# Projections from three products of rounded parts, with rows exchanged by transfers within SBUF

## The reference

```python
x = x + gnn(layernorm(x), adj, ...)          # ends in elu(hidden @ W_out + b_out)
h = rmsnorm(layernorm(x), g1)                # [2048, 512]
q, k, v = split(h @ w_qkv, 3)                # w_qkv [512, 1536], fp32
q, k = rope(q, cos, sin), rope(k, cos, sin)  # out_r = xr*c - xi*s, out_i = xr*s + xi*c
y = softmax(causal(q @ k.T / sqrt(32))) @ v  # 16 heads of 32
x = x + y @ w_o
x = x + moe(rmsnorm(x, g2), w_router, w1, w2)   # top 2 of 8 experts, capacity 640
```

## Time and profile before

| | us |
|---|---|
| median of 3 runs | 2176.4 (2174.52 to 2177.14) |
| the profiled execution | 2175.5 |
| its span | 2173.8 |
| TensorE busy | 2023.7 (93%) |
| VectorE busy | 1539.4 (71%) |
| ScalarE busy | 1100.1 (51%) |
| GpSimd busy | 717.8 (33%) |

### The profile page before, as it was taken

How to read it: one execution, slowest core, us unless ns; L and a number is a source line. 1 busy time by engine, 2 the same in 40 slices (tenths; PEclk the granted TensorE clock), 3 DMA queues, 4 the chain that set the end, 5 groups by cost and what they waited for, 6 DMA issues and landing times. The chain is left out here.

```text
span 2173.8 us, 41935 instructions
## 1 busy us (share of the span) xinstructions
PE 2023.7 (93%) x17522; PEld 1202.1 (55%) x17522; DVE 1539.4 (71%) x2484; ACT 1100.1 (51%) x1088; POOL 717.8 (33%) x503
## 2 busy tenths in 40 slices
PE   6899999999999999999999999998991999999997
PEld 3554444444444444554444444444440799999996
DVE  7889999989995766768778778677558544444442
ACT  5778989898893433223454545444440423332321
POOL 3410000000000011335797879877440322222211
PEclk9999999999999999999999999999995999999999
DMA  7421212121213312343104031010222544444431
GB/s 272 155 82 54 72 53 79 49 77 51 74 52 106 138 49 74 140 148 90 40 7 111 21 86 32 25 40 13 76 91 99 189 126 125 99 116 126 126 64 25
DMA packets 92393, 187.70 MB, mean 86 GB/s; under 512 B 14924, under 2 KB 24140, under 8 KB 87820
## 3 DMA queue, kind: packets, MB, share of 16 engines
q1 hardware_dynamic: 83244, 164.04, 22.9%
q0 software_dynamic: 8960, 20.98, 5.2%
HBM read 139.25 MB, written 41.28 MB: 83 GB/s over the span
## 5 line engine op out<-in xcount | busy, mean ns | idle before, releaser
L1782 DVE TENSOR_REDUCE t_rm<-t_m 128x1 f32<-128x512 f32 (+3 forms) x640 | 371.9, 605 | 125.8 <-PE t_m L1923 81.1
L1707 ACT ACTIVATE t_E<-t_s 128x1024 f32<-128x1024 f32 (+3 forms) x320 | 277.3, 895 | 351.9 <-PE t_s L1940 196.3
L629 ACT ACTIVATE m_step<-m_ub,gat_bias 128x2048 bf16<-128x2048 f32 x128 | 250.0, 1989 | 13.9 <-DMA m_ub<-scratch_uac 8.5
L773 PE MATMUL m_bd<-m_mask,m_S 128*32 128x512 bf16 x3072 | 230.3, 379 | 10.9 <-DVE m_mask L719 10.9
L773 PE MATMUL m_bd<-gat_adjT,m_S 128*32 128x512 bf16 x2496 | 201.4, 379 | 4.8 <-PE m_dn L773 4.8
L2135 POOL DMA_INDIRECT out<-e_ye,e_token x40 | 80.7, 2017 | 330.5 <-DVE e_ye L2257 325.8
L966 POOL MEMSET k_triq<- 128x128 bf16 x1 | 0.2, 205 | 572.5 <-POOLq L2391 572.5
L773 PE MATMUL m_bd<-m_mask,m_neg 128*32 128x512 bf16 x2496 | 188.9, 379 | 0.0
L2320 PE MATMUL e_h<-e_xTh,e_w1h 128*128 128x320 f32 x512 | 158.4, 309 | 0.8 <-DVE e_xTl L2236 0.8
L2320 PE MATMUL e_h<-e_xTh,e_w1l 128*128 128x320 f32 x512 | 158.2, 309 | 0.0
L2320 PE MATMUL e_h<-e_xTl,e_w1h 128*128 128x320 f32 x512 | 158.2, 309 | 0.0
(11 more groups left out here) (385 smaller groups left out, 4404.0 us busy)
## 6 DMA issues: line engine op xcount, KB each, us to landing
a_adj<-in_adj SPq DMA_DIRECT2D x16, 1024.0 KB, 5.0
m_ub<-scratch_uac SPq DMA_DIRECT2D x16, 1024.0 KB, 5.0
e_w1r<-in_L_ffn_w SPq DMA_DIRECT2D x8, 2048.0 KB, 9.7
e_w2r<-in_L_ffn_w SPq DMA_DIRECT2D x8, 2048.0 KB, 9.3
tq_Q<-scratch_parts SPq DMA_DIRECT2D x36, 256.0 KB, 4.5
gat_scale<-scratch_uac SPq DMA_DIRECT2D x32, 256.0 KB
scratch_parts<-o_hi SPq DMA_DIRECT2D x32, 256.0 KB, 2.2
scratch_parts<-o_lo SPq DMA_DIRECT2D x32, 256.0 KB, 2.7
```

Of the source, the lines that this page charges most:

```text
L629: act.activation(step(n), ub[h % 2][:, :].rearrange("p (t q) -> p t q", t=T), ACT.Relu, bias=bias[:, j, h:h + 1], scale=BIG).then_inc(step ...
L773: return pe.matmul(out[c * TILE:(c + 1) * TILE, :], lhs, rhs[:, c * BANK:(c + 1) * BANK], **flags)
L1707: act.activation(E[n % 3][:, two, off:BANK], ps_s[:, two, off:BANK], ACT.Exp, scale=SCALE).then_inc(exp_done[z], 1)
L1782: dve.tensor_reduce(rm[:, h, t, ch:ch + 1], ps_m[i % 2][:, 0:w], AX, ALU.max).then_inc(entry_read, 1)
```

## The change

Everything is in stage_front.

- Wr holds the raw weights of w_qkv. ScalarE writes their scaled and rounded high part Wh (weight_high), VectorE the rest Wl (weight_low): 12 pieces of 128x512 each, by the tables HIGHS and LOWS behind the output products. The transposes too are split, into xT[0] by ScalarE and xT[1] by VectorE (turned_low), for two chunks at a time.
- A projection is 12 products (PRODUCTS) with fp32r operands instead of four in fp32. The router's weights G are split into Gs; its products have 16 and 8 columns, into a bank of their own, behind each v item.
- ORDER is another: the Q and K projections of chunk 0 come first, V later; the last chunk ends in qk, qk, v, v. Projections have three banks instead of four.
- The shuffle on VectorE is gone. SP exchanges neighbouring rows from raw to swap with two transfers within SBUF (exchange(n)), and the store of item n-3 stands ahead of it in SP's list. raw has three buffers.
- A rotation follows one item behind its projection, high and low parts two items behind it.
- The tables of cosines and sines are loaded by chunks; load_first stands before item 24.

```diff
-    BANKS = 4
+    BANKS = 3
+    PRODUCTS = ((0, 0), (0, 1), (1, 0))
...
+    ORDER = outs(0, 5) + [("var", 0), ("norm", 0)] + outs(5, 6) + turns(0)[0:2] + outs(6, 7) + turns(0)[2:4] + [qk[0]]
+    ORDER += outs(7, 8) + [qk[1]] + outs(8, 9) + [("var", 1), ("norm", 1), qk[2]] + outs(9, 10) + [qk[3]] + outs(10, 11)
+    ORDER += turns(1) + [qk[4]] + outs(11, 12) + [vs[0]] + outs(12, 13) + [("var", 2), ("norm", 2), qk[5]] + outs(13, 14)
+    ORDER += [vs[1]] + outs(14, 15) + [qk[6]] + outs(15, 16) + [vs[2], qk[7], vs[3]] + turns(2) + [qk[8]]
+    ORDER += [("var", 3), ("norm", 3), vs[4], qk[9], qk[10], vs[5], qk[11], qk[12], vs[6], qk[13], qk[14], vs[7], qk[15]]
+    ORDER += turns(3)
+    for c in (2, 3):
+        q, t = qk[8 * c:8 * c + 8], vs[4 * c:4 * c + 4]
+        ORDER += q[0:2] + t[0:1] + q[2:4] + t[1:2] + q[4:6] + (t[2:3] if c == 2 else []) + q[6:8] + t[3 if c == 2 else 2:]
...
+    HIGHS = {1: ((0, 0), (0, 1)), 2: ((0, 2), (0, 3)), 4: ((1, 0),), 5: ((1, 1),), 6: ((1, 2),), 7: ((1, 3),),
+             8: ((2, 0),), 9: ((2, 1),), 10: ((2, 2), (2, 3))}
+    LOWS = {2: ((0, 0), (0, 1)), 3: ((0, 2), (0, 3)), 6: ((1, 0),), 7: ((1, 1),), 8: ((1, 2),), 9: ((1, 3),),
+            10: ((2, 0), (2, 1)), 11: ((2, 2), (2, 3))}
...
+                def exchange(n):
+                    sp.wait_ge(evicted, PLACE[("qk", n)] + 1)
+                    if n >= 3:
+                        sp.wait_ge(parts_ready, n - 2)
+                    for z in range(2):
+                        sp.dma_start(swap[n % 3][z:P:2, :], raw[n % 3][1 - z:P:2, :]).then_inc(swapped[n % 3], 16)
...
+                for n in range(len(QK)):
+                    if n >= 3:
+                        store(n - 3)
+                        if n in (10, 18):
+                            load_turns(2 + (n - 10) // 8)
+                    if n == 24:
+                        load_first()
+                    exchange(n)
+                for n in range(len(QK) - 3, len(QK)):
+                    store(n)
...
-                    dve.wait_ge(evicted, PLACE[("qk", n)] + 1)
-                    if n >= 3:
-                        dve.wait_ge(parts_ready, n - 2)
-                    lk(dve.stream_shuffle(swap[n % 3][:, :], raw[r][:, :], [d ^ 1 for d in range(32)]))
-                    lk(dve.tensor_tensor(swap[n % 3][:, :], swap[n % 3][:, :], S[:, c * BANK:(c + 1) * BANK], ALU.mult))
+                    dve.wait_ge(swapped[n % 3], 32 * (n // 3 + 1))
+                    dve.wait_ge(cs_in[c % 2], 32 * (c // 2 + 1))
+                    lk(dve.tensor_tensor(swap[n % 3][:, :], swap[n % 3][:, :], S[:, c % 2, :], ALU.mult))
...
+                def weight_low(m, k):
+                    dve.wait_ge(w_high[m], k + 1)
+                    cut = slice(m * D, (m + 1) * D)
+                    dve.scalar_tensor_tensor(Wl[:, k, cut], Wr[:, k, cut], gcol[:, k:k + 1],
+                                             Wh[:, k, cut].bitcast(F32), ALU.mult, ALU.subtract).then_inc(scaled[m], 1)
+
+                def turned_low(n):
+                    dve.wait_ge(t_high, n + 1)
+                    cut = slice(n % 4 * P, (n % 4 + 1) * P)
+                    dve.tensor_tensor(xT[1][:, n // 4 % 2, :, cut], ps_t[n % 2][:, :].rearrange("p (k q) -> p k q", q=P),
+                                      xT[0][:, n // 4 % 2, :, cut].bitcast(F32), ALU.subtract).then_inc(t_ready, 1)
...
                 for kind, n in ORDER:
+                    if kind in ("out", "qk", "v"):
+                        if to_split:
+                            low_part(to_split.pop(0))
+                        if to_rotate:
+                            rotate(to_rotate[0])
+                            to_split.append(to_rotate.pop(0))
+                    if kind == "qk":
+                        to_rotate.append(n)
                     if kind == "out":
                         before_exp(n)
                         if n:
                             residual(n - 1)
+                        for m, k in LOWS.get(n, ()):
+                            weight_low(m, k)
...
+                    if kind == "turn":
+                        turned_low(n)
...
                         for k in range(KD):
-                            mm = pe.matmul(ps[i % BANKS][:, :], Wq[:, k, m * D + g * P:m * D + (g + 1) * P],
-                                           xgT[:, k, c * BANK:(c + 1) * BANK], start=(k == 0), stop=(k == KD - 1))
+                            for z, (wp, xp) in enumerate(PRODUCTS):
+                                mm = pe.matmul(ps[i % BANKS][:, :], W[wp][:, k, m * D + g * P:m * D + (g + 1) * P],
+                                               xT[xp][:, c % 2, k, :], start=(k == 0 and z == 0), stop=(k == KD - 1 and z == 2))
```

More of the change, by code:

```diff
@@ L897, in stage_front @@
         lo = [st.sb(f"lo{i}", [P, BANK], F32R) for i in range(2)]
+        gcol, stats = st.sb("gcol", [P, 8]), st.sb("stats", [P, T, 6])
+        ve, sd = st.sb("ve", [P, 2, T]), st.sb("sd", [P, 2, T])
+        Gs = st.sb("Gs", [P, KD, 2 * EXPERTS], F32R)
+        st.sb("gap", [P, 64])
+        st.sb("place_of_Wo", [P, KD * D])
+        with Stage(nc, "o") as place:
+            Wr = place.sb("wr", [P, KD, 3 * D])
+        Wl = st.sb("wl", [P, KD, 3 * D], F32R)
+        xT = [st.sb(f"xT{n}", [P, 2, KD, BANK], F32R) for n in ("h", "l")]
+        W = (Wh, Wl)
+        raw.append(st.sb("raw2", [P, BANK]))
+        brow = st.sb("brow", [P, D])
         ps_s = [st.ps(f"s{i}", [P, BANK]) for i in range(2)]
@@ L991, in evict @@
                     act.wait_ge(job_full, PLACE[("qk", n)] + 1)
[L992 to L995 removed]
+                    if n >= 3:
+                        act.wait_ge(cos_done, n - 2)
+                        act.wait_ge(swapped[n % 3], 32 * (n // 3))
+                    act.activation(raw[n % 3][:, :], ps[PLACE[("qk", n)] % BANKS][:, :], ACT.Copy).then_inc(evicted, 1)
                 def root(g):
@@ L1031, in _ @@
                         act.activation(V[:, n, :], ps[PLACE[("v", n)] % BANKS][:, :], ACT.Copy).then_inc(evicted, 1)
-                    if kind in ("out", "qk", "v") and waiting:
-                        high(waiting.pop())
-                    if kind == "qk":
-                        waiting.append(n)
+                for n in waiting:
+                    high(n)
             @block.vector
@@ L1108, in _ @@
                         normalise(n)
-                    if kind == "qk":
-                        if cs:
-                            dve.wait_ge(cs_in, 32)
-                            cs = False
-                        rotate(n)
-                    if kind in ("out", "qk", "v") and waiting:
-                        low_part(waiting.pop())
-                    if kind == "qk":
-                        waiting.append(n)
+                    if kind == "turn":
+                        turned_low(n)
+                for n in to_split:
+                    low_part(n)
+                for n in to_rotate:
+                    rotate(n)
+                    low_part(n)
                 prob, ratio = keep["prob"], ve[:, 0, :]
```

137 lines of the change are left out of this document (72 added, 65 removed).

## The result

| | before | after |
|---|---|---|
| median | 2175.5 (2174.5 to 2177.1) | 2198.6 (2196.3 to 2199.5) |
| the profiled execution | 2175.5 | 2198.4 |
| its span | 2173.8 | 2196.5 |
| start of stage_front | 695.38 | 695.01 |
| first product of the attention | 949.87 | 957.41 |

The changed kernel is slower: the ratio of the times is 1.0104, with an interval of 1.0086 to 1.0121. The forecast was 2178.8, in a range of 2162 to 2193. The table splits the 22.7 us of the span: 7.5 are there when the attention begins, of which the forecast had 2.4. The other 15.2 arise behind the stage, where the forecast had none.

The account below looks back on a forecast made before the run. The prediction took the stage to be bound by TensorE: 31 us saved against 33.6 to 34.6 us spent on idle time, lower clock, end and transposes, a shift of 2.4 us to 2178.8, range 2162 to 2193.

Parts of the forecast that it names:

- Gaps 1 to 4: TensorE idle before the first transposes, projection 0, the third transpose of tiles 4 to 7, V projection 0: 5.0, 4.5, 13.5, 6.2 us.
- The walk on VectorE: Stage's work followed in each engine's list order; VectorE is the chain from exchange 0's landing at 744.7 to V projection 0.
- The lower clock behind the new gaps: TensorE runs at its lower clock behind three gaps in the stage, costing 3 x 2.8 us.
- The products: Each projection as 12 single-pass products of 0.232 us takes 2.79 us instead of 3.44; 31 us of TensorE work goes.
- The exchange: Two 128 KB transfers within SBUF on SP's queue land 2.65 us after the eviction's end, range 1.8 to 3.3.
- The steady stretch holds: From projection 8 on: high part ends 5.4 us after its projection, two projections take 5.6, three banks of slack.
- gaps behind 840: Sign against the forecast: TensorE gaps after 840 us would mean the steady stretch is wrong.
- The end: Behind the last rotated projection a 9.15 us chain against 8.1 us of TensorE work; next stage at 952.3, 2.4 us later.
- Nothing behind this stage changes: The stages from the attention on keep their time: 0 us of change there.
- The rule weighed: VectorE's two-input multiply beside GpSimd's is 0.3 to 0.4 us longer, not blocked; five collisions cost 1.2 us, not 6.5.
- The shorter chain: Rival: exchanges land in 1.8 us and VectorE's chain is shorter than the walk; 2168 us, chance 0.25.
- The slow exchange: Rival: the exchange pair needs 4.6 us, adding 2 us at five exchanges and at the end; 2191 us, chance 0.2.

Follow-up runs that it names:

- e4_gap_fillers: The changed kernel with filler products on TensorE in its four gaps (5, 5, 14 and 6 of 0.86 us each), the end as it is: 2190.5 us, ratio 1.0071.
- e1_end_filler: The changed kernel with 11 filler products of 0.86 us instead of one on TensorE at the end of the stage: 2188.7 us, ratio 1.0055.
- e2_before_idle: The kernel before with 13 copies on ScalarE behind its last eviction, about 8.5 us without work for TensorE before the attention: 2197.7 us, ratio 1.0102.
- g1_loads_back: The changed kernel reordered, with more projections between output products, fillers in the first two gaps, and the attention's six loads ahead of exchange 26: 2191.5 us, ratio 1.0063.
- g2_order_spread: The spread order: g1_loads_back with the weights' low parts placed anew, norm 3 two projections earlier and a few projections swapped with output products: 2177.1 us, ratio 0.9999.

## Why the prediction was wrong

**Gaps 1 to 4: right.** Forecast 5.0, 4.5, 13.5 and 6.2 us, measured 5.09, 4.72, 12.96 and 6.14. Projection 8 was forecast at 836.65 and started at 833.3; TensorE's last product was forecast to end at 950.75 and ended at 948.8. The walk on VectorE with its durations from the earlier trace rows holds to 0.6 us in each gap and to some 3 us in time (833.3 for 836.65).

**The lower clock behind the new gaps: right.** 3 x 2.8 = 8.4 us forecast, and e4_gap_fillers gave 8.1 back.

**The products: right.** Their pitch is 0.231 us (929.65 to 929.88), forecast 0.232 from the earlier trace rows.

**The exchange: right in size, but not everywhere.** 2.1 us at the median from issue to landing, with 1.1 us of issue for the pair. Behind the six loads it took up to 6.0 us. The prediction had asked only whether their issue fits into SP's list.

**"The steady stretch holds": wrong.** The step compared a latency (5.4 us from projection to high part) with a pace (5.6 us for two projections) and counted on three banks. It left out that ScalarE's list is strict: an eviction stands behind a high part that waits for VectorE. It also left out that the eviction itself starts the GpSimd multiply which then holds VectorE up. One turn of that takes 3.8 us, not 2.8. In the profile most of the backlog was there before that, through the exchanges and stores that landed late beside the loads. The three banks don't absorb it; they only hide it from TensorE until nothing follows that could catch up. I had written that gaps behind 840 would speak against this step; TensorE has hardly any there, and the step was wrong all the same. The idle time of the bottleneck doesn't show a backlog that builds up behind it.

**The end: too short by 5.1 us.** Forecast 952.3, measured 957.4. The chain behind the last eviction is close: 9.15 us forecast from the end of the projection to the landing and 9.65 to the next stage, with 0.65 for the eviction. Measured from the eviction's start at 946.40 to 957.2 it is 10.8. The eviction started 5.9 us behind its projection. That is the mis-sized term.

**"Nothing behind this stage changes": wrong, and the dearest.** It cost 15.2 us, of which at least 12.8 went through the clock (e1_end_filler). I had read the lower clock at the first gap and put 2.8 us on it, and the forecast had 2.4 us more of end. I took the price of a fallen clock from dense work and never asked what stands behind the last gap. The work there holds a high clock but doesn't regain it.

**The rule weighed: wrongly decided.** I read the earlier trace rows as a two-input multiply that takes 0.3 to 0.4 us longer beside GpSimd's. That was the mean over 32 of them. One of them, before:

```profile
903.47 1.28 POOL L961 TENSOR_TENSOR o_spun<-o_raw,o_cos 128x512 f32<-128x512 f32 x1 [3.05 <-ACT o_raw L995]
904.20 1.09 DVE L1085 TENSOR_TENSOR o_swap<-o_swap,o_sin 128x512 f32<-128x512 f32 x1
```

VectorE began 0.73 us into GpSimd's instruction, behind its shuffle, so that little was left to wait for. The rows after decide it: started 0.08 us behind GpSimd, L1128 takes 1.76 us and ends 0.55 us after GpSimd's multiply (945.11 against 944.56). Nearly all of its own 0.69 us lies behind GpSimd's end. The Trainium skill (SBUF — State Buffer, section SBUF: two separate sides) says just that, an exclusive lock for the whole instruction, and these rows agree with it. Its price in the walk was small all the same: up to V projection 0 two low parts took 1.76 us instead of 0.69, 2.1 us together. In the whole stage it is more than the multiplies show: against 0.69 us each, three of these, four additions and three low parts are longer by some 9 us in all (an estimate from the means 772, 813 and 779 ns of 32 each). At the end it closed the circle.

**The rivals.** The shorter chain and the slow exchange both moved VectorE's gaps, and those were right. The slow exchange put 2 us more on the stage's end; none had the late eviction there, or the clock behind it.

## What to carry to other kernels

When a change makes the bottleneck's work shorter, follow the other engines' lists to the end of the stage, at their own pace, and ask what drains there: slack in buffers hides a backlog until the last item. Price an idle time of TensorE by the work that follows it. In the kernel before, 8.5 us of idle time added ahead of the attention cost 22 us, and in the kernel after ten more dense products in the gap bought 10 us back, five behind it 6.6. A version that looks equal to its baseline can hide a gain behind such a clock: the spread order was level at 2177 and 0.6% faster once the 4.3 us of idle time at its end and two smaller gaps were filled.

## What was unexpected of the hardware

- The granted clock stayed at 0.50 for 43 us of TensorE busy at 99%, after 8.57 us of idle time; 4.18 and 3.72 us of idle time were enough for the same, 0.85 us and 0.45 us were not. Five 128x512 products of 128 rows ended it in some 4 us.
- The same 3.00 us of idle time lowered the clock in the kernel before and didn't in e2_before_idle. In g1_loads_back and g2_order_spread it fell 1.5 and 0.7 us after TensorE had begun to work again.
- Rows of 128 KB exchanged within SBUF by two transfers (every other partition) land 2.1 us from issue at the median, 1.9 to 6.0 in the stage, and cost SP 0.55 us of issue each, against 0.73 us of VectorE for the shuffle.
- A store of 256 KB takes 2.2 to 2.7 us to land, but 7 to 8 us when six loads of 256 KB are issued beside it.
